# A graph layer on one core: the first mixture panel and the Q tiles, loaded by ScalarE's queue instead of SyncE's

## What is computed

```
x = x + gnn(xn) + mix(xn)          # gnn: h = xn @ W.T + b, then a normalised sum over 20000 edges
q, k, v = heads(xn @ Wq.T + bq), heads(xn @ Wk.T + bk), heads(xn @ Wv.T + bv)
kv   = einsum('bhsm,bhsd->bhmd', relu(k P) / 8, v)
mix  = merge(einsum('bhsm,bhmd->bhsd', relu(q P) / 8, kv)) @ Wo.T + bo
x = x + experts(layernorm(x))      # 8 gated experts with routing weights
```

## Time and profile before

| | us |
|---|---|
| median of 3 runs | 1086.49 |
| lowest, highest | 1084.27, 1086.54 |
| the profiled execution's own time | 1084.87 |
| its span, from the first to the last instruction | 1083.1 |
| TensorE busy | 1062.4 (98%) |
| VectorE busy | 536.7 (50%) |
| GpSimd busy | 349.5 (32%) |
| ScalarE busy | 290.0 (27%) |
| mean granted TensorE clock | 0.995 |

### The profile page before, as it was taken

How to read it: one execution, slowest core, us unless ns; L and a number is a source line. 1 busy time by engine, 2 the same in 40 slices (tenths; PEclk the granted TensorE clock), 3 DMA queues, 4 the chain that set the end, 5 groups by cost and what they waited for, 6 DMA issues and landing times.

```text
span 1083.1 us, 15216 instructions
## 1 busy us (share of the span) xinstructions
PE 1062.4 (98%) x5527; PEld 882.0 (81%) x5527; DVE 536.7 (50%) x1152; ACT 290.0 (27%) x445; POOL 349.5 (32%) x225
## 2 busy tenths in 40 slices
PE   8999999999999999999959999999999999999998
PEld 7887778887878888888848888887788888888887
DVE  6944666676641222332427657967334212214684
ACT  5320211112232234321222223267222212202221
POOL 4000011122130025375500249955108744500151
PEclk9999999999999999999989999999999999999999
DMA  7303011222233386645595567766045556205912
GB/s 270 98 30 108 13 35 53 62 69 72 70 121 88 141 313 244 234 146 174 169 324 207 204 189 215 197 170 183 1 161 196 206 179 218 64 24 224 378 66 110
DMA packets 135933, 163.17 MB, mean 151 GB/s; under 512 B 8534, under 2 KB 102578, under 8 KB 130738
## 3 DMA queue, kind: packets, MB, share of 16 engines
q1 hardware_dynamic: 135282, 160.33, 44.9%
q10 hardware_dynamic: 576, 1.84, 0.4%
HBM read 107.70 MB, written 54.45 MB: 150 GB/s over the span
## 4 chain that ended last, share of the span: by engine, by line
PE 94%; DVE 3%; DMA 1%; SPq 1%; ACT 1%; issue 1%; ACTq 0%
PE ps L1890 9%; PE ps L1892 9%; PE ps L1891 9%; PE ps L2225 7%; PE ps L2226 7%; PE ps L2227 7%; PE ps L2136 6%; PE ps L2137 6%; PE ps L2138 6%; PE ps L2159 4%; PE ps L2165 4%; PE ps L2056 3%; PE ps L2058 3%; PE ps L2057 3%; PE ps L1900 2%; PE ps L2002 2%
## 5 line engine op out<-in xcount | busy, mean ns | idle before, releaser
L1890 PE MATMUL ps<-w_hi,xnH 128*128 128x512 f32 x464 | 184.6, 398 | 0.0
L1892 PE MATMUL ps<-w_hi,xnL 128*128 128x512 f32 x464 | 180.9, 390 | 0.0
L1891 PE MATMUL ps<-w_lo,xnH 128*128 128x512 f32 x464 | 180.7, 389 | 0.0
L892 POOL TENSOR_TENSOR acc<-acc,cw 128x320 f32<-128x320 f32 x40 | 35.7, 893 | 252.6 <-ACT cw L1096 251.4
L1890 PEld LDWEIGHTS ps<-w_hi,xnH 128*128 128x128 f32 x464 | 87.1, 188 | 18.7
L1892 PEld LDWEIGHTS ps<-w_hi,xnL 128*128 128x128 f32 x464 | 87.1, 188 | 18.6
L1891 PEld LDWEIGHTS ps<-w_lo,xnH 128*128 128x128 f32 x464 | 87.2, 188 | 17.1
L1841 DVE TENSOR_TENSOR prd<-ps,wB 128x512 f32<-128x512 f32 (+1 forms) x24 | 14.2, 593 | 144.5 <-PE ps L2227 105.4
L2056 PE MATMUL ps<-xnH,w_hi 128*128 128x512 f32 (+1 forms) x192 | 68.1, 355 | 0.0
L2225 PE MATMUL ps<-x2H,guH 128*128 128x512 f32 (+1 forms) x192 | 67.7, 352 | 0.4 <-ACT wT L1334 0.4
L2226 PE MATMUL ps<-x2L,guH 128*128 128x512 f32 (+1 forms) x192 | 67.6, 352 | 0.0
(11 more groups left out here) (474 smaller groups left out, 2243.8 us busy)
## 6 DMA issues: line engine op xcount, KB each, us to landing
cR<-c_d SPq DMA_DIRECT2D x20, 640.0 KB, 5.0
foldin<-in SPq DMA_DIRECT2D x32, 256.0 KB, 2.7
guR<-in SPq DMA_DIRECT2D x16, 512.0 KB, 6.8
w_raw<-in SPq DMA_DIRECT2D x14, 512.0 KB, 6.3
c_d<-cw SPq DMA_DIRECT2D x40, 160.0 KB
wdq<-in SPq DMA_DIRECT2D x6, 1024.0 KB, 7.6
qR<-qT_d SPq DMA_DIRECT2D x20, 256.0 KB, 4.9
wd_d<-wd1H SPq DMA_DIRECT2D x5, 1024.0 KB, 6.5
```

Source lines behind the costliest of these rows:

```text
L1890: pe.matmul(target, xnH[:, kc, cols], wH[w][:, kc, :], start=(kc == 0), stop=False)
L1891: pe.matmul(target, xnH[:, kc, cols], wL[w][:, kc, :], start=False, stop=False)
L1892: mm = pe.matmul(target, xnL[:, kc, cols], wH[w][:, kc, :], start=False, stop=(kc == KC - 1))
```

## The change

`load_mix_panel(0)` and all ten `load_q(t)` leave SP's order. ScalarE issues them instead: the panel behind `h_high(0, 9)` and the steps of the panel chain that stand there, and `load_q(t)` behind `h_high(1, t)` and the chain's steps there. The waits ahead of the DMAs are the same as before, on other engines. SP keeps `load_mix_panel(1)`, now right behind the chain.

```diff
-            def load_q(t):
-                sp.wait_ge(*made(("h", 1, t)))
-                cols = slice(t * P, (t + 1) * P)
-                for k in range(2):
-                    sp.dma_start(qR[k][:, :, cols], qT_d[4 * k:4 * k + 4, :, cols].rearrange("k q n -> q k n"))\
-                      .then_inc(in_q[t // HALF], 16)
...
-            sp.wait_ge(*made(("h", 0, NT - 1)))
-            load_mix_panel(0)
-            for t in range(NT - 1):
-                load_q(t)
             load_mix_panel(1)
-            load_q(NT - 1)
...
+            def load_first_panel():
+                act.wait_ge(*made(("h", 0, NT - 1)))
+                for part in range(2):
+                    act.dma_start((mwH, mwL)[part][0][:].bitcast(F32), m_d[0, part, :, 0:4, :]).then_inc(in_w[0][part], 16)
+
+            def load_q(t):
+                act.wait_ge(*made(("h", 1, t)))
+                cols = slice(t * P, (t + 1) * P)
+                for k in range(2):
+                    act.dma_start(qR[k][:, :, cols], qT_d[4 * k:4 * k + 4, :, cols].rearrange("k q n -> q k n"))\
+                       .then_inc(in_q[t // HALF], 16)
...
                     for n in MIX_AT.get(NT * hf + t, ()):
                         mix_high(n)
+                    if hf == 0 and t == NT - 1:
+                        load_first_panel()
+                    if hf:
+                        load_q(t)
```

## The result

| | before | after |
|---|---|---|
| median, us | 1085.06 | 1088.79 |
| lowest to highest of 9 runs each | 1084.27 to 1086.54 | 1087.06 to 1090.03 |
| the profiled execution, its span | 1084.87, 1083.1 | 1090.03, 1088.2 |
| mean granted TensorE clock | 0.995 | 0.992 |

A forecast was written before the change was run, and what follows sets the result against it. TensorE's 11.1 us wait for late Q-tile DMAs ahead of the first product was taken as the bound; 7.85 us earlier start plus 1.64 of clock gave 9.5 us, 1086.49 to 1077.0, range 1073.5 to 1082.

The forecast's parts named there:

- The reading of before: Ahead of the first product (L2136): 11.1 us of waiting is bandwidth spent too late, with room for it earlier.
- SP's second panel and the tiles 5 to 9 need no care: Behind the chain: panel 1 competes with tiles 4 to 8, but only tile 4 is needed for the first token.
- The wait at h's eighth tile: In h's second half: TensorE waits 1.8 us for the bank that a delayed htmp drains.
- 1.0 us for a pair of issues: ScalarE's order: each DMA issue takes 0.5 us, a pair 1.0, since its queue holds little until 536.
- the signs of being wrong: First token's split waiting for a Q tile, ScalarE issues over 1 us, chain ending after 545, or chain not delayed.
- X: Delay at the end of the mixed-panel chain from the added traffic: 3.0 us, from four legs at 0.75.
- The bound of 15 us: Upper bound of the chain's delay: each extra transfer holds a leg for its whole time, 4.2 MB at 280 GB/s.
- Rival C: Chain stretched at its bound: from 10.9 us first product no earlier than 559.25; 15 gives 563.4, 1091 us; chance 0.05.
- Rival B: ScalarE's queue fills from 538: one issue ahead of the tokens costs 3 us more, gain 6.5, 1080; chance 0.09.
- the prediction's steps from the last mixH split: ScalarE behind the chain: h tiles, then issue pairs of 1.0 us, up to the first token's split at 548.8.
- With a wait under 4 us the clock should not fall: TensorE's clock at the first product: the shortened wait keeps it up, gaining 1.64 us.
- rival D: DMA engines' rate binds, not issue order; another transfer lands at 556 or so instead: no gain, 1086.5; chance 0.05.

The follow-up runs named there:

- e10: e8 with tiles 0 and 1 behind the store of step 12, tiles 2, 3, 4 behind those of steps 13, 14, 15: 1075.32 us (before 1085.46).
- e6: Kernel before plus 22 DMAs of 8 KB into a spare tensor, issued at the change's places on ScalarE: 1086.01 us (before 1085.67).
- e1: The change with all Q tiles back on SP behind the chain, only the first panel on ScalarE: 1084.17 us (before 1085.33).
- e1b: Kernel before with the first panel issued earlier on SP, ahead of the block's load in the same queue: 1084.62 us (before 1085.33).
- e3: The change with Q tiles 5 to 9 issued by SP behind the chain again: 1082.41 us (before 1085.33).
- e2: The change with the first panel back on SP behind the chain, only the Q tiles on ScalarE: 1089.53 us (before 1085.33).
- e5: e4 plus, on SP, tiles 0 to 2 behind the store of step 12, 3 and 4 behind that of step 15: 1078.50 us (before 1085.67).
- e4: Kernel before with the first panel issued earlier on SP, right behind the block's load and the mixH store: 1082.83 us (before 1085.67).
- e8: e5 with the chain's last three steps one or two tiles of h later in ScalarE's order: 1078.49 us (before 1085.57).

## Why the prediction was wrong

**What held.** The reading of before held: the 11.1 us were bandwidth spent too late, room for it lies under the chain, and it is worth about 10 us (e10). That SP's second panel and the tiles 5 to 9 need no care held behind the second product only, from where the two profiles keep a constant distance (5.0 there, 5.1 at the end); ahead of it this traffic was under way while ScalarE's issues stood still. The wait at h's eighth tile was foretold at its place and by its mechanism, the bank that waits for htmp behind ScalarE, with 1.8 us instead of 5.5. And 1.0 us for a pair of issues holds where little is under way (0.93 to 1.12 for the pairs of tiles 0 to 4 in the change, mostly 1.1 to 1.25 in e6). Of the signs of being wrong, two came: a chain that ends after 545 (546.16) and issues over 1 us.

**What failed first: X.** The step is "sharing doubles only the wire time ... four at 0.75. X = 3.0". Measured was 10.9. It was wrong in two ways. The smaller one is the count: the prediction names five legs (a load, three stores, a load) and adds up four; five met extra traffic, which at its own price gives 3.75. The larger one is the price: a leg lost 1.0 to 2.3 us beside a pair of tiles (0.2 to 2.0 against e6) and 5.2 beside the panel (5.5), not 0.75. The leg was taken to share the engines with the big transfer. But it landed when the big transfer did: at 511.2 against 511.0 in the change, 512.2 against 512.1 in e1 (504.62 + 7.6; 500.97 + 11.1), 510.9 against 510.1 in e1b (503.17 + 7.7; 500.94 + 9.2). The bound of 15 us that stood beside the estimate was the nearer end, and the reason given for the lower one, a DMA share of 0.40 before the change, didn't bear it out. Rival C's threshold, a stretch of 10.9, is where the stretch landed, but the first product was not at C's 559.25 for it. That it was at 563.32, where C had it for X = 15 (563.4), is a coincidence: it is 10.9 of stretch and 4.2 of what comes next.

**What failed second: a pair is 1.0 on ScalarE.** For the pairs of tiles 7 and 8 it was 5.69 and 3.22 us, while the second panel and ScalarE's own earlier pairs were under way (DMA share 1.03 from 548 to 552). Rival B had the mechanism, and its price of 3 us for one issue; there were two such pairs. The first split came at 560.71; with the stretch alone and the prediction's steps from the last mixH split, 10.3 us, it would have come at 556.5. B is the other 4.2 us by this working. Measured with e3, which takes it away, it is more: the first product is then at 556.82, 6.5 earlier, at the end of h. Rivals B and C had been priced as if each came alone, and they came together. Whether the longer chain also made the issues slower, by bringing more transfers into the same few microseconds, no run separates: in e2, with half the stretch but the first panel there too, the longest pair took 10.38.

**What failed third: the clock.** "With a wait under 4 us the clock should not fall" is contradicted by e10: 2.4 us of waiting, and from 552.01 the matmuls take 0.63 instead of 0.40, 1.5 us after TensorE has restarted; the first product takes 4.09 us instead of 2.72. In e5 the clock is 0.74 in 540 to 544, behind a wait of 3.5. But in e1 it stayed at 1.00 from 540 to 552, with a wait of 2.6 at h's tile. Nor is there one time from a stop to the fall: from the stretches it is about 4.1 us before, 2.6 in the change and 2.0 in e3 (TensorE stops at 538.0, and the mean clock of 538 to 540 is 0.99, that of the next 2 us 0.50). And one kernel's executions differ: e10's four runs have mean clocks of 0.998, 0.997, 1.000 and 0.999, and the last two, at 1074.43, are 1.8 us faster than the profiled one (how long TensorE waited in them isn't known). So the length of the wait alone doesn't say whether the clock falls; where it did, in e10's profile, it cost the first product 1.4 us.

**Sharing between queues.** The Trainium skill (DMA: Bandwidth & Descriptors, Queues, rings and completion order) says that an engine goes round its queues a packet at a time. No run here shows a small transfer served sooner for being in a queue of its own: 7.6 us in one of its own (e1), 7.7 behind the panel in the same one (e1b).

The Trainium skill (DMA: Bandwidth & Descriptors, Issuing engines are not separate DMA queues) says that DMAs from several engines run on the same 16 and that a second issuer saves only issue time. e1 and e1b agree with it: 0.5 us between them in median, within their intervals. It had spoken for rival D, nothing. In the change the issue time was not saved but moved onto ScalarE, where two pairs took 8.9 us.

## What stays open

Why a leg waits for nearly all of the 2 MB, instead of taking a share of each engine from its start, isn't settled: e1 and e1b show that it doesn't depend on the queue, and e4 that it depends, for the most part, on what was issued first, but no run varied the size or the number of pieces of the big transfer. Nor was it tried whether Q tiles, which come in pieces of 512 bytes, weigh more than their 256 KB. e10's places were not tried without its change of ScalarE's order. Stretches and waits are from one execution of each kernel, so that differences under about 1 us between two of them say little.

## What to carry to other kernels

A chain of small stores and loads that wait for one another looks like room for other transfers, but a leg can lose most of the duration of what is issued just ahead of it (5.2 us here). Issue large transfers behind a leg (e4 against e1b), spread tiles over several legs, and see what else waits for the chain's stores (e10 against e8). DMAs issued by an engine that computes were cheap here while the DMA engines had room and held that engine's work when they were full, so count on it only for issues ahead of the rush (e3). Price rivals that can come together also as a sum: here one gave 10.9 us of stretch and the other 4.2 to 6.5 us more.

## What the runs showed of the hardware that was not expected

- A load of 256 KB that lands after 3.3 us in the kernel before lands after 7.5, 7.6 and 7.7 us when 2 MB were issued some 3 us ahead of it, in the other queue or its own (the change, e1, e1b), and after 3.7 when they were issued 0.8 us behind it (e4).
- One pair of issues of 256 KB each on ScalarE took between 0.93 us (the change) and 10.38 us (e2, with 4 MB of panels issued just before).
- The granted clock fell 1.5 us after a restart behind a wait of 2.4 us (e10), 2.0 us after TensorE stopped in e3, and not at all in a wait of 2.6 us (e1).
